# Second context's column sums from k-tiles added in 16 bits on GpSimd and VectorE, in place of 64 column-tiled matmuls

## The chip, the core and the metric

The kernel runs on one core of a Trainium2 chip. The metric is the device time of one execution in microseconds (us). Three runs of the kernel before gave 602.07, 602.37 and 602.42 us; the median is 602.37 us.

## The reference

Two residual blocks over x, of shape (2, 1024, 2048); each of the two batch entries has its own context of 2048 x 2048.

```python
def fake_quant(x, scale, zp):
    q = jnp.clip(jnp.round(x / s + z), 0.0, 255.0)
    return (q - z) * s
# first block: both operands quantised, then a matmul with the context
x = x + jnp.tanh(g_xattn[0]) * jnp.matmul(fake_quant(_layernorm(x)), fake_quant(ctx_4096))
# second block: a linear layer of rank 512
weight = U * S[None, :] @ V.T
x = x + jnp.tanh(g_ffn[0]) * jnp.einsum('bti,oi->bto', _layernorm(x), weight)
```

The zero points are not whole numbers that can be taken out beforehand, so the matmul runs on centred integers, which bf16 holds exactly, and the rest is repaired by a row correction and a column correction. The column correction needs, for each of the 2048 columns of a context, the sum over its 2048 rows (k) of the quantised context.

## The kernel before

**Tiling.** Rows of x go in 16 tiles (t or u, 0 to 15) of 128 rows; tiles 0 to 7 belong to the first context, 8 to 15 to the second. Columns go in four blocks n of 512. The contraction k has 16 tiles of 128. `q2` holds one quantised context in bf16, [128, 4, 16, 512]; the second overwrites the first. A context arrives in chunks of two k-tiles (128 x 1024): eight chunks to a column block, 32 to a context. Chunks are numbered 0 to 31 and 32 to 63. So the second context's blocks n = 0, 1, 2, 3 are chunks 32-39, 40-47, 48-55, 56-63.

**Stages of a tile.** `s1(t)` is the first matmul (four units of 16 matmuls, L556), `x1_unit` adds it to the rows in `ring`; `mm3(u)` (L587, L592) and `mm4(u)` (L653, L654, L658) are the two halves of the low-rank layer, with operands split in f16 high and low parts; `hid_hi`/`hid_lo` and `x_hi`/`x_lo` make those splits on ScalarE and VectorE; `y_unit` adds the result (L1207). Every engine's queue is written out by hand, in order; semaphores are the only ordering between engines.

**The second context.** ScalarE loads and rounds each chunk to uint8 into a ring `u8r` of eight places (`op1`, L757), and waits for the chunk eight earlier to have been converted. GpSimd converts each chunk to centred bf16 in `q2` (`op2`, L254); all 32 chunks of the second context are GpSimd's. ScalarE's last two roundings (chunks 62, 63) stand behind `hid_hi(7)`. After the 32 conversions GpSimd does `pre_row(8)` (L260) and `pre(8, n)` (L265).

**Its column sums.** On TensorE, between `mm4(6)` and `mm4(7)`, `colsum(1, n)` for n = 0, 1, 2 runs 48 matmuls in column-tiled form: ones of 128 x 32 against a k-tile, four k-tiles at a time into four groups of 32 partitions (L523). Block 3's 16 follow behind `mm4(7)`. Each bank then holds four partial sums. ScalarE and VectorE split them into f16 high and low parts (`column_parts` L840, `column_low` L1195) in `corr`, and `colsum_total` (L532, L533) adds the groups by two matmuls to a block: for blocks 0 to 2 inside `mm4(7)`, for block 3 behind the first unit of `s1(8)`. ScalarE writes the correction (`column_correction`, L851), which GpSimd adds to the rows of tiles 8 to 15.

**Order on VectorE around there:** `xT_copy(1)`, `quantise(8)` (L1107), `hid_lo(7)` (L1190), `row_correction(8)`, `y_unit(6, 0..3)` with `sums1(9)` and `variance1(9)` in between, `column_low(0..2)`, `quantise(9)`, `y_unit(7, 0..3)` and the rest of tiles 9 and 10.

Of the kernel before, what the change touches and what calls it, by code (L numbers as in the profile page):

```python
# [7 lines left out]
def gated_block_program(nc, x, ctx_in, params, U_t, S, V, out):  # L8
# [4 lines left out]
    P = 128  # L13
    NB, SEQ, D = x.shape
    RANK = V.shape[1]
    KT = D // P
    RT = RANK // P
    W = 512
# [5 lines left out]
    CQ = KT // CK  # L24
    CB = NQ * CQ
    R = 4
    G = 3
    NST = 10
    CG = 4
    GW = P // CG  # L30
    H_PE = (5,)
# [15 lines left out]
    with es:  # L47
# [98 lines left out]
        colsum_done = sem("colsum_done")  # L146
        parts_hi = sem("parts_hi")
        parts_lo = sem("parts_lo")
        colsum_summed = sem("colsum_summed")
        corr_ready = sem("corr_ready")  # L150
# [44 lines left out]
        unit_bank = lambda t, n: bank[4 * (n % 2) + t] if t < G else bank[(unit(t, n) - NQ * G) % 3]  # L195
        colsum_bank = lambda b, n: bank[4 * (n % 2) + 3] if b == 0 else bank[n]
        h_bank = lambda u: bank[3 + u % 2]
# [4 lines left out]
        y_bank = lambda i: bank[5 + i % 3]  # L202
        part_hi = lambda n: corr[:, n * W:n * W + W // 2].bitcast(f16)
        part_lo = lambda n: corr[:, n * W + W // 2:(n + 1) * W].bitcast(f16)
        chunk = lambda c: (c // CB, c % CB // CQ, c % CQ)
# [34 lines left out]
        def _(pool):  # L240
            def op2(c):
# [10 lines left out]
                if b > 0:  # L252
                    pool.wait_ge(s1_done, unit(TB * b - 1, n) + 1)
                nc.gpsimd.tensor_scalar(q2_chunk(c), u8r[:, c % NU8, :], C_NC2, 1.0, ALU.add, ALU.mult)\  # L254
                    .then_inc(q2_pool, 1)

            def pre_row(t):
                pool.wait_ge(q_u8, part_count(t))
                pool.wait_ge(row_ready, t + 1)
                nc.gpsimd.tensor_scalar(xt(t), xt(t), bvec[:, t % R, 1:2], 1.0, ALU.add, ALU.mult).then_inc(x1_row, 1)  # L260

            def pre(t, n):
# [10 lines left out]
                                    base=0, pattern=[[-1, P]], channel_multiplier=1).then_inc(ident_ready, 1)  # L273
            nc.gpsimd.memset(ones_h[:, :], 4.0 / GW).then_inc(setup_ready, 1)

# [12 lines left out]
            for t in range(G, NT):  # L288
                if t == TB:
                    for c in range(CB, 2 * CB):  # L290
                        op2(c)
                if t == G:
                    pool.wait_ge(t_written, 2 * G)
                    nc.gpsimd.memset(ident_h, 0.0).then_inc(ident_free, 1)
                    pool.wait_ge(ident_free, 1)
                    nc.gpsimd.affine_select(out=ident_h, in_=ident_h, compare_op=ALU.not_equal, fill=1.0, base=0,
                                            pattern=[[-1, P]], channel_multiplier=1).then_inc(ident_ready, 1)
                if t not in (6, 7):
                    pre_row(t)
                    for n in range(NQ):  # L300
                        pre(t, n)
                elif t == 6:
                    for v, n in MIXED:
                        if n == 0:
                            pre_row(v)
                        pre(v, n)
# [182 lines left out]
        def _(pe):  # L489
# [15 lines left out]

            def colsum(b, n, k0=0, k1=KT):
                if k0 == 0 and b == 0 and n >= 2:
                    pe.wait_ge(corr_ready, n - 1)
                if k0 == 0 and b > 0:
                    if n < NQ - 1:  # L510
                        pe.wait_ge(x1_ready, S1_END(TB - 1))
                    else:
                        pe.wait_ge(h_hi, TB - 1)
                        pe.wait_ge(h_lo, TB - 1)
                for k in range(k0, k1):
                    if k % CK == 0:
                        need_chunk(CB * b + CQ * n + k // CK)
                    if b == 0:
                        mm = nc.tensor.matmul(colsum_bank(b, n)[:, :], ones_b[:, :], q2[:, n, k, :],  # L519
                                              start=(k == 0), stop=(k == KT - 1))  # L520
                    else:
                        g = k % CG * GW
                        mm = nc.tensor.matmul(colsum_bank(b, n)[g:g + GW, :], ones_b[:, g:g + GW], q2[:, n, k, :],  # L523
                                              start=(k < CG), stop=(k >= KT - CG), tile_position=(0, g))
                if k1 == KT:
                    mm.then_inc(colsum_done, 1)

            def colsum_total(n):
                pe.wait_ge(setup_ready, 5)
                pe.wait_ge(parts_hi, n + 1)  # L530
                pe.wait_ge(parts_lo, n + 1)
                nc.tensor.matmul(colsum_bank(1, n)[:, :], ones_h[:, :], part_hi(n), start=True, stop=False)  # L532
                nc.tensor.matmul(colsum_bank(1, n)[:, :], ones_h[:, :], part_lo(n), start=False, stop=True)\  # L533
                    .then_inc(colsum_summed, 1)

# [83 lines left out]
            def mm4(u):  # L619
# [4 lines left out]
                for n in range(NQ):  # L624
# [8 lines left out]
                    if u == 0:  # L633
                        pe.wait_ge(split_hi, VP + RT * (n + 1))
                    if u == TB - 1 and n == 2:
                        for j in range(NQ - 1):
                            colsum_total(j)
                    t_hi, t_lo = hT_of(u)[:, 0:RT, :], hT_of(u)[:, RT:2 * RT, :]
# [35 lines left out]
            pe.wait_ge(ident_ready, 1)  # L674
            colsum(0, 0, 0, CK)
            q_pieces(0, 0)
            q_pieces(0, 1)
            colsum(0, 0, CK, 2 * CK)
            s1_part(0, 0, 0, 2 * CK)
            colsum(0, 0, 2 * CK, 3 * CK)  # L680
            s1_part(0, 0, 2 * CK, 3 * CK)
# [3 lines left out]
            for i in range(3, 7):  # L685
                if i == 6:
                    q_pieces(2, 0)
                colsum(0, 0, CK * i, CK * i + CK)
                for t in range(2):
                    s1_part(t, 0, CK * i, CK * i + CK)  # L690
            q_pieces(2, 1)
            s1_part(2, 0, 0, 7 * CK)
            colsum(0, 0, 7 * CK, KT)
            for t in range(G):
                s1_part(t, 0, 7 * CK, KT)
            for n in range(1, NQ):
                for i in range(CQ):
                    colsum(0, n, CK * i, CK * i + CK)
                    for t in range(G if n < NQ - 1 else 1):
# [29 lines left out]
            mm4(6)  # L729
            for n in range(NQ - 1):  # L730
                colsum(1, n)
            mm4(7)
            colsum(1, NQ - 1)
            s1_part(8, 0)
            colsum_total(NQ - 1)
            for n in range(1, NQ):
# [12 lines left out]
        def _(act):  # L749
# [84 lines left out]

            def column_parts(n):
                act.wait_ge(colsum_done, NQ + n + 1)
                act.wait_ge(x1_pre, unit(TB - 1, n) + 1)
                if n == 0:
                    act.wait_ge(ctx_u8, act_u8(CORR_CHUNK))
                nc.scalar.activation(part_hi(n), colsum_bank(1, n)[:, :], ACT.Copy, scale=0.25).then_inc(parts_hi, 1)  # L840

            def column_correction(b, n):
                if b > 0:
                    act.wait_ge(colsum_summed, n + 1)
                else:
                    act.wait_ge(colsum_done, n + 1)
                    if n == 0:
                        act.wait_ge(const_ready, 1)
                    elif n == NQ - 1:
                        act.wait_ge(smax_ready, 1)  # L850
                nc.scalar.activation(corr[:, n * W:(n + 1) * W], colsum_bank(b, n)[:, :], ACT.Identity,  # L851
# [158 lines left out]
            for n in range(NQ - 1):  # L1010
                column_parts(n)
            for n in range(NQ - 1):
                column_correction(1, n)
            op2(9)
            column_parts(3)
            column_correction(1, 3)
# [17 lines left out]
        def _(dve):  # L1034
# [130 lines left out]
            def x_lo_half(u, g):  # L1165
                mean, scale = ln2[:, u % 2, 0:1], ln2[:, u % 2, 8:9]
                if 2 * u + g > 0:
                    dve.wait_ge(xs_lo, 2 * u + g)
                if u == 6 and g == 0:
                    dve.wait_ge(ctx_u8, act_u8(XN_CHUNK))  # L1170
# [21 lines left out]

            def column_low(n):
                dve.wait_ge(parts_hi, n + 1)
                stt(part_lo(n), colsum_bank(1, n)[:, :], 0.25, part_hi(n), ALU.mult, ALU.subtract).then_inc(parts_lo, 1)  # L1195

# [186 lines left out]
            xT_copy(1)  # L1383
            quantise(8)
            hid_lo(7)
            row_correction(8)
            y_unit(6, 0)
            y_unit(6, 1)
            sums1(9)
            variance1(9)  # L1390
            y_unit(6, 2)
            y_unit(6, 3)
            column_low(0)
            column_low(1)
            column_low(2)
            quantise(9)
            y_unit(7, 0)
            y_unit(7, 1)
            row_correction(9)
            sums1(10)  # L1400
            y_unit(7, 2)
            y_unit(7, 3)
            column_low(3)
            variance1(10)
# [59 lines left out]
```

## Time and profile before

| | us |
|---|---|
| median of 3 runs (range) | 602.37 (602.07 to 602.42) |
| profiled execution: its span | 600.8 |
| TensorE matmuls busy | 583.0 (97%) |
| VectorE busy | 384.5 (64%) |
| ScalarE busy | 210.5 (35%) |
| GpSimd busy | 193.5 (32%) |

The profile gives the span of its execution, from the first instruction to the last. The time of the same execution is not listed apart; the median of the runs is 1.5 us above the span. Busy is the time in which an engine had an instruction under way. A matmul's record overlaps the next one's, so the distance between starts, not the record's length, is what one costs. "Idle before" a row is the gap ahead of it and the event that ended the gap.

### The profile page before, as it was taken

What the parts mean: (1) busy time and instruction counts of PE and PEld (TensorE: products, weight loads), DVE (VectorE), ACT (ScalarE), POOL (GpSimd) and SP (SyncE); (2) the same over time, 40 slices, a digit from 0 to 9 for tenths busy, and PEclk for the clock granted to TensorE, in tenths of its full rate; (3) what the DMA queues carried; (4) which work ended last, traced back from release to release, by engine and by line L of the source; (5) the groups of instructions that cost most, each with busy time, mean ns of one, the idle gap of its engine ahead of it and who ended that gap; (6) DMA issues with size and microseconds to landing.
All of it is one profiled execution on the core that took longest, in us unless ns stands there. A gap on an engine that the chain in (4) does not pass through costs nothing.

```text
span 600.8 us, 7536 instructions
## 1 busy us (share of the span) xinstructions
PE 583.0 (97%) x2800; PEld 266.3 (44%) x2800; DVE 384.5 (64%) x703; ACT 210.5 (35%) x256; POOL 193.5 (32%) x149
## 2 busy tenths in 40 slices
PE   1999999999999999999999999999999999999998
PEld 0444444444444444445444444444444444444444
DVE  6968999995288962855266975647375665735212
ACT  4799877822041432476422220303011030301000
POOL 2998850002223419735505800210404030030000
PEclk9999999999999999999999999999999999999999
DMA  8999995539828896979934432360917355171512
GB/s 275 387 387 386 308 262 127 109 122 196 242 54 230 192 217 189 274 264 327 235 123 140 102 73 54 75 189 12 211 42 157 106 97 166 32 161 35 123 53 105
DMA packets 145940, 102.74 MB, mean 171 GB/s; under 512 B 108784, under 2 KB 109040, under 8 KB 145904
## 3 DMA queue, kind: packets, MB, share of 16 engines
q1 hardware_dynamic: 136912, 84.96, 53.6%
q10 hardware_dynamic: 8992, 17.30, 8.8%
q8 instruction: 22, 0.36, 0.2%
q14 instruction: 14, 0.11, 0.1%
HBM read 58.99 MB, written 16.78 MB: 126 GB/s over the span
## 4 chain that ended last, share of the span: by engine, by line
PE 74%; DVE 12%; DMA 7%; issue 3%; ACT 1%; SPq 1%; POOL 1%; ACTq 0%; DVEq 0%
PE bank L556 27%; PE bank L587 14%; PE bank L654 8%; PE bank L653 8%; PE bank L658 8%; PE bank L592 7%; DMA v_hl<-in_ctx_dram 4%; DVE u_hl L1249 2%; DVE ring L1134 2%; DVE xn L1171 1%; DVE xs L1174 1%; DVE v_hl L1243 1%; DMA qT<-qn 1%; PE bank L519 1%; DMA ring<-in_x_dram 1%
## 5 line engine op out<-in xcount | busy, mean ns | idle before, releaser
L556 PE MATMUL bank<-q,qT 128*128 128x512 bf16 x896 | 202.1, 381 | 0.6 <-DVE ring L1134 0.3
L556 PEld LDWEIGHTS bank<-q,qT 128*128 128x128 bf16 x896 | 87.7, 98 | 107.9 <-issue 1.8
L260 POOL TENSOR_SCALAR ring<-ring,bvec 128x2048 f32<-128x2048 f32 x16 | 33.3, 2084 | 270.2 <-DVE bvec L1116 270.2
L587 PE MATMUL bank<-v_hl,xT 128*128 128x512 f16 x512 | 115.8, 379 | 0.0
L265 POOL TENSOR_TENSOR ring<-ring,corr 128x512 f32<-128x512 f32 x64 | 88.7, 1417 | 24.6 <-ACT corr L851 23.6
L1134 DVE SCALAR_TENSOR_TENSOR ring<-bank,const,ring 128x512 f32<-128x512 f32 x64 | 47.6, 743 | 57.9 <-PE bank L556 57.8
L1207 DVE SCALAR_TENSOR_TENSOR ring<-bank,cy,ring 128x512 f32<-128x512 f32 x63 | 46.6, 747 | 56.7 <-PE bank L658 56.6
L654 PE MATMUL bank<-u_hl,hbuf 128*128 128x512 f16 x208 | 78.9, 380 | 0.0
L653 PE MATMUL bank<-u_hl,hbuf 128*128 128x512 f16 x208 | 78.9, 379 | 0.0
L254 POOL TENSOR_SCALAR q<-u8r,const 128x1024 bf16<-128x1024 uint8 x52 | 64.2, 1243 | 39.2 <-ACT u8r L757 35.6
L587 PEld LDWEIGHTS bank<-v_hl,xT 128*128 128x128 f16 x512 | 49.9, 98 | 59.9 <-DMA xT<-xs 0.5
L798 ACT ACTIVATE ln<-ln,const 128x1 f32<-128x1 f32 x16 | 4.7, 294 | 189.8 <-DVE ln L1147 189.8
L592 PE MATMUL bank<-v_hl,xT 128*128 128x512 f16 x256 | 60.5, 379 | 0.0
L658 PE MATMUL bank<-u_hl,hbuf 128*128 128x512 f16 x208 | 53.4, 379 | 0.0
L1174 DVE TENSOR_TENSOR xs<-xn,xs 128x1024 f16<-128x1024 f32 x32 | 46.8, 1461 | 5.3 <-ACT xs L812 4.3
L1136 DVE BATCH_NORM_STATS2 st<-ring 128x6 f32<-128x512 f32 x64 | 44.5, 695 | 2.2
L1075 DVE BATCH_NORM_STATS2 st<-ring 128x6 f32<-128x512 f32 x64 | 40.4, 680 | 8.2 <-DMA ring<-in_x_dram 8.1
L812 ACT ACTIVATE xs<-ring,ln 128x1024 f16<-128x1024 f32 x32 | 38.2, 1232 | 14.8 <-DVE ln L1159 14.8
L592 PEld LDWEIGHTS bank<-v_hl,xT 128*128 128x128 f16 x256 | 25.1, 98 | 30.2
L784 ACT ACTIVATE qn<-qn,const 128x2048 bf16<-128x2048 uint8 x13 | 26.0, 2002 | 29.3 <-DVE qn L1107 29.3
L1190 DVE SCALAR_TENSOR_TENSOR hbuf<-bank,hbuf 128x512 f16<-128x512 f32 x16 | 11.0, 686 | 34.3 <-ACT hbuf L826 34.3
L519 PE MATMUL bank<-q,ones_b 128*128 128x512 bf16 x64 | 20.4, 402 | 12.7 <-POOL q L254 12.1
(136 smaller groups left out, 524.9 us busy)
## 6 DMA issues: line engine op xcount, KB each, us to landing
out_dram<-ring SPq DMA_DIRECT2D x63, 256.0 KB, 3.6
ring<-in_x_dram SPq DMA_DIRECT2D x62, 256.0 KB, 4.1
v_hl<-in_ctx_dram SPq DMA_DIRECT2D x26, 512.0 KB, 11.5
stage<-in_ctx_dram ACTq DMA_DIRECT2D x17, 512.0 KB, 5.5
u_hl<-in_L_ffn_V_dram SPq DMA_DIRECT2D x8, 512.0 KB, 11.4
corr<-in_ctx_dram ACTq DMA_DIRECT2D x8, 512.0 KB, 6.1
stage<-in_ctx_dram SPq DMA_DIRECT2D x6, 512.0 KB, 11.4
q<-in_ctx_dram ACTq DMA_DIRECT2D x4, 512.0 KB, 10.1
```

Of the source, the lines that this page charges most:

```text
L254: nc.gpsimd.tensor_scalar(q2_chunk(c), u8r[:, c % NU8, :], C_NC2, 1.0, ALU.add, ALU.mult)\
L265: nc.gpsimd.tensor_tensor(xq(t, n), xq(t, n), corr[:, n * W:(n + 1) * W], ALU.add).then_inc(x1_pre, 1)
L556: mm = nc.tensor.matmul(unit_bank(t, n)[:, :], qT_of(t)[:, k, :], q2[:, n, k, :], start=(k == 0), stop=(k == KT - 1))
L587: nc.tensor.matmul(h_bank(u)[:, :], xT[:, g, half, k % 8, :], v_hl[:, k, 0, :], start=(g == 0 and a == 0 and half == 0), stop=False)
L592: mm = nc.tensor.matmul(h_bank(u)[:, :], xT[:, g, 0, k % 8, :], v_hl[:, k, 1, :], start=False, stop=(g == 1 and a == 7))
L653: nc.tensor.matmul(y_bank(i)[:, :], t_hi[:, r, :], u_hl[:, n, r, 0, :], start=(r == 0), stop=False)
L654: nc.tensor.matmul(y_bank(i)[:, :], t_lo[:, r, :], u_hl[:, n, r, 0, :], start=False, stop=False)
L658: mm = nc.tensor.matmul(y_bank(i)[:, :], t_hi[:, r, :], u_hl[:, n, r, 1, :], start=False, stop=(r == RT - 1))
L1134: stt(xq(t, n), unit_bank(t, n)[:, :], C_A, xq(t, n), ALU.mult, ALU.add).then_inc(x1_ready, 1)
L1136: nc.vector.bn_stats(st2[:, t % R, n, :], xq(t, n)).then_inc(st2_ready, 1)
L1174: tt(xs[:, g, 1, :], xn[:, :], xs[:, g, 0, :], ALU.subtract).then_inc(xs_lo, 1)
L1207: stt(xq(u, n), y_bank(i)[:, :], cy[:, n:n + 1], xq(u, n), ALU.mult, ALU.add).then_inc(y_ready, 1)
```

## The change

The 64 column-tiled matmuls and the split in parts go. Instead the eight chunks of a column block are added element by element into one 128 x 1024 sum in f16 (seven additions to a block; a chunk's two k-tiles stay side by side), and two full-width matmuls with ones add the two halves and the 128 partitions. GpSimd makes the sums of blocks 0 and 1: after each conversion of a chunk of blocks 2 and 3 except the first of each, it adds a chunk of block 0 or 1. VectorE makes those of blocks 2 and 3. The sums lie in `xn` (blocks 0, 1) and in the low halves of `xs` (blocks 2, 3). On TensorE the sums of blocks 0, 1, 2 stand between `mm4(6)` and `mm4(7)`, that of block 3 behind the first unit of `s1(8)`. VectorE's `sums1(9)`, `variance1(9)`, `quantise(9)`, `row_correction(9)` and `sums1(10)` move by a place or two.

The index in `k_sum` reads c = CB + CQ * n + i, the chunk i of block n. In GpSimd's loop the call has n = 0 while chunks 48 to 55 are converted and n = 1 while chunks 56 to 63 are.

```diff
+    KS = CQ - 1
+        k_sums = lambda n: xn[:, n * W:n * W + W].bitcast(f16) if n < 2 else xs[:, n // 3, 0, :]
...
+            def k_sum(n, i):                                   # GpSimd
+                c = CB + CQ * n + i
+                if i == 1:
+                    pool.wait_ge(q2_pool, pool_count(c))
+                    pool.wait_ge(xs_lo, 2 * TB)
+                else:
+                    pool.wait_ge(k_summed_pool, KS * n + i - 1)
+                nc.gpsimd.tensor_tensor(k_sums(n), q2_chunk(c - 1) if i == 1 else k_sums(n), q2_chunk(c), ALU.add)\
+                    .then_inc(k_summed_pool, 1)
...
-            nc.gpsimd.memset(ones_h[:, :], 4.0 / GW).then_inc(setup_ready, 1)
+            nc.gpsimd.memset(ones_h[:, :], 1.0).then_inc(setup_ready, 1)
...
                     for c in range(CB, 2 * CB):
                         op2(c)
+                        if c >= CB + 2 * CQ and c % CQ > 0:
+                            k_sum((c - CB) // CQ - 2, c % CQ)
...
-            def colsum_total(n):
+            def colsum_of_sums(n):                             # TensorE
                 pe.wait_ge(setup_ready, 5)
+                if n < 2:
+                    pe.wait_ge(k_summed_pool, KS * (n + 1))
+                else:
+                    pe.wait_ge(k_summed, KS * (n - 1))
+                if n < 2:
+                    pe.wait_ge(xT_copied, 4)
+                else:
+                    pe.wait_ge(h_hi, TB - 1 + n - 2)
+                    pe.wait_ge(h_lo, TB - 1 + n - 2)
+                for a in range(CK):
+                    mm = nc.tensor.matmul(colsum_bank(1, n)[:, :], ones_h[:, :], k_sums(n)[:, a * W:(a + 1) * W],
+                                          start=(a == 0), stop=(a == CK - 1))
+                mm.then_inc(colsum_done, 1)
...
-                    if u == TB - 1 and n == 2:
-                        for j in range(NQ - 1):
-                            colsum_total(j)
...
             mm3(7)
             mm4(6)
-            for n in range(NQ - 1):
-                colsum(1, n)
+            colsum_of_sums(0)
+            colsum_of_sums(1)
+            colsum_of_sums(2)
             mm4(7)
-            colsum(1, NQ - 1)
             s1_part(8, 0)
-            colsum_total(NQ - 1)
+            colsum_of_sums(3)
...
-            def column_parts(n):                               # ScalarE
             def column_correction(b, n):
+                act.wait_ge(colsum_done, NQ * b + n + 1)
+                if b > 0:
+                    act.wait_ge(x1_pre, unit(TB - 1, n) + 1)
+                    if n == 0:
+                        act.wait_ge(ctx_u8, act_u8(CORR_CHUNK))
...
-            def column_low(n):                                 # VectorE
+            def k_sum(n, i):
+                c = CB + CQ * n + i
+                dve.wait_ge(q2_pool, pool_count(c))
+                if i == 1:
+                    dve.wait_ge(xT_written, 2 + 2 * (n // 3))
+                else:
+                    dve.wait_ge(k_summed, KS * (n - 2) + i - 1)
+                tt(k_sums(n), q2_chunk(c - 1) if i == 1 else k_sums(n), q2_chunk(c), ALU.add).then_inc(k_summed, 1)
...
             xT_copy(1)
             quantise(8)
+            k_sum_part(2, 1, 4)
             hid_lo(7)
             row_correction(8)
             y_unit(6, 0)
+            k_sum_part(2, 4, 6)
             y_unit(6, 1)
+            k_sum_part(2, 6)
+            y_unit(6, 2)
             sums1(9)
             variance1(9)
-            y_unit(6, 2)
             y_unit(6, 3)
-            column_low(0)
-            column_low(1)
-            column_low(2)
+            k_sum_part(3, 1, 4)
+            y_unit(7, 0)
+            k_sum_part(3, 4, 6)
             quantise(9)
-            y_unit(7, 0)
             y_unit(7, 1)
+            k_sum_part(3, 6)
+            y_unit(7, 2)
             row_correction(9)
+            y_unit(7, 3)
             sums1(10)
-            y_unit(7, 2)
-            y_unit(7, 3)
-            column_low(3)
```

`k_sum_part(n, a, b)` calls `k_sum(n, i)` for i from a to b - 1 (to 7 where b is left out). `x_lo_half(8, 0)` gets a wait for all eight column sums, since `xn` is its room.

## Rows read from the trace of the kernel before

**Rows 1.** The page, parts 1 and 2: engine totals, and TensorE's granted clock by slice.

```profile
PE 583.0 (97%) x2800; PEld 266.3 (44%) x2800; DVE 384.5 (64%) x703; ACT 210.5 (35%) x256; POOL 193.5 (32%) x149
...
PEclk9999999999999999999999999999999999999999
```

**Rows 2.** Waits of TensorE over the span: total us, times, longest us.

```profile
PE bank L519 <- POOL q L254: 12.1, 2, 11.3
...
PE bank L556 <- DVE ring L1134: 0.3, 1, 0.3
```

**Rows 3.** Timeline of TensorE: start us, us, instruction, [idle before].

```profile
304.16 1.03 PE L658 MATMUL bank<-u_hl,hbuf 128*128 128x512 f16 x4
305.12 2.77 PE L523 MATMUL bank<-q,ones_b 128*32 128x512 bf16 x48
307.82 0.39 PE L653 MATMUL bank<-u_hl,qT 128*128 128x512 f16 x1
...
318.62 1.03 PE L658 MATMUL bank<-u_hl,qT 128*128 128x512 f16 x4
319.58 1.05 PE L523 MATMUL bank<-q,ones_b 128*32 128x512 bf16 x16
320.56 3.63 PE L556 MATMUL bank<-q,qT 128*128 128x512 bf16 x16
```

**Rows 4.** Timeline of GpSimd through the last conversions of the second context.

```profile
266.57 1.12 POOL L254 TENSOR_SCALAR q<-u8r,const 128x1024 bf16<-128x1024 uint8 x1 [3.48 <-ACT u8r L757]
268.32 1.12 POOL L254 TENSOR_SCALAR q<-u8r,const 128x1024 bf16<-128x1024 uint8 x1 [0.63 <-ACT u8r L757]
...
286.91 3.17 POOL L254 TENSOR_SCALAR q<-u8r,const 128x1024 bf16<-128x1024 uint8 x2 [0.63 <-ACT u8r L757]
296.68 2.25 POOL L254 TENSOR_SCALAR q<-u8r,const 128x1024 bf16<-128x1024 uint8 x2 [6.60 <-ACT u8r L757]
```

**Rows 5.** Timeline of ScalarE: the rounding of chunk 49.

```profile
265.25 1.23 ACT L757 ACTIVATE u8r<-corr,par,const 128x1024 uint8<-128x1024 f32 x1
```

**Rows 6.** Single lines on GpSimd: duration ns min/median/max, first and last start, form.

```profile
L265 POOL TENSOR_TENSOR ring<-ring,corr x64: 1260/1271/2255, 42.7 to 530.1; 128x512 f32<-128x512 f32 x64
...
L254 POOL TENSOR_SCALAR q<-u8r,const x52: 1111/1118/2077, 10.1 to 297.8; 128x1024 bf16<-128x1024 uint8 x52
...
L260 POOL TENSOR_SCALAR ring<-ring,bvec x16: 1971/1972/2515, 32.2 to 524.4; 128x2048 f32<-128x2048 f32 x16
```

**Rows 7.** Timeline of GpSimd at the start: a conversion that waits for its predecessor.

```profile
13.81 1.19 POOL L245 TENSOR_SCALAR u8r<-v_hl,const,par 128x1024 uint8<-128x1024 f32 x1 [2.62 <-DMA v_hl<-in_ctx_dram]
15.09 1.12 POOL L254 TENSOR_SCALAR q<-u8r,const 128x1024 bf16<-128x1024 uint8 x1
```

**Rows 8.** Single lines on VectorE, columns as in rows 6.

```profile
L1174 DVE TENSOR_TENSOR xs<-xn,xs x32: 1224/1226/2872, 82.3 to 552.9; 128x1024 f16<-128x1024 f32 x32
...
L1184 DVE COPY xT<-bank x4: 681/682/692, 272.8 to 284.9; 128x1024 f16<-128x1024 f16 x4
```

**Rows 9.** Timelines of GpSimd and VectorE where both are at work.

```profile
336.72 6.38 POOL L265 TENSOR_TENSOR ring<-ring,corr 128x512 f32<-128x512 f32 x4
...
339.79 2.18 DVE L1174 TENSOR_TENSOR xs<-xn,xs 128x1024 f16<-128x1024 f32 x1
```

**Rows 10.** Timeline of VectorE in the stretch of the new additions.

```profile
265.45 1.22 DVE L1174 TENSOR_TENSOR xs<-xn,xs 128x1024 f16<-128x1024 f32 x1 [1.81 <-ACT xs L812]
...
286.65 1.34 DVE L1107 TENSOR_SCALAR qn<-ring,ln 128x2048 uint8<-128x2048 f32 x1
295.49 0.69 DVE L1190 SCALAR_TENSOR_TENSOR hbuf<-bank,hbuf 128x512 f16<-128x512 f32 x1 [7.49 <-ACT hbuf L826]
```

**Rows 11.** Timeline of TensorE at its start.

```profile
17.10 1.91 PE L556 MATMUL bank<-q,qT 128*128 128x512 bf16 x4
...
20.65 1.63 PE L496 MATMUL bank<-ident_b,qn 128*128 128x128 bf16 x16
22.82 1.47 PE L556 MATMUL bank<-q,xT 128*128 128x512 bf16 x6 [0.54 <-ACT xT L789]
```

More of the change, by code:

```diff
@@ L28, in gated_block_program @@
     NST = 10
-    CG = 4
-    GW = P // CG
     H_PE = (5,)
@@ L146, in gated_block_program @@
         colsum_done = sem("colsum_done")
-        parts_hi = sem("parts_hi")
-        parts_lo = sem("parts_lo")
-        colsum_summed = sem("colsum_summed")
+        k_summed = sem("k_summed")
+        k_summed_pool = sem("k_summed_pool")
         corr_ready = sem("corr_ready")
@@ L195, in gated_block_program @@
         unit_bank = lambda t, n: bank[4 * (n % 2) + t] if t < G else bank[(unit(t, n) - NQ * G) % 3]
-        colsum_bank = lambda b, n: bank[4 * (n % 2) + 3] if b == 0 else bank[n]
+        colsum_bank = lambda b, n: bank[4 * (n % 2) + 3] if b == 0 else bank[(0, 1, 3, 4)[n]]
         h_bank = lambda u: bank[3 + u % 2]
@@ L202, in gated_block_program @@
         y_bank = lambda i: bank[5 + i % 3]
-        part_hi = lambda n: corr[:, n * W:n * W + W // 2].bitcast(f16)
-        part_lo = lambda n: corr[:, n * W + W // 2:(n + 1) * W].bitcast(f16)
+        k_sums = lambda n: xn[:, n * W:n * W + W].bitcast(f16) if n < 2 else xs[:, n // 3, 0, :]
         chunk = lambda c: (c // CB, c % CB // CQ, c % CQ)
@@ L504, in need_chunk, with colsum @@
                     pe.wait_ge(q2_pool, pool_count(c))
-            def colsum(b, n, k0=0, k1=KT):
-                if k0 == 0 and b == 0 and n >= 2:
+            def colsum(n, k0=0, k1=KT):
+                if k0 == 0 and n >= 2:
                     pe.wait_ge(corr_ready, n - 1)
[L509 to L514, printed above, removed]
@@ L515, in colsum @@
                 for k in range(k0, k1):
                     if k % CK == 0:
[L517 to L524, printed above, removed]
+                        need_chunk(CQ * n + k // CK)
@@ L525, in colsum @@
+                    mm = nc.tensor.matmul(colsum_bank(0, n)[:, :], ones_b[:, :], q2[:, n, k, :],
+                                          start=(k == 0), stop=(k == KT - 1))
                 if k1 == KT:
                     mm.then_inc(colsum_done, 1)
-            def colsum_total(n):
+            def colsum_of_sums(n):
                 pe.wait_ge(setup_ready, 5)
[L530 to L534, printed above, removed]
+                if n < 2:
[11 more added lines that the diff above has]
+                mm.then_inc(colsum_done, 1)
@@ L674, in _ @@
             pe.wait_ge(ident_ready, 1)
-            colsum(0, 0, 0, CK)
+            colsum(0, 0, CK)
             q_pieces(0, 0)
             q_pieces(0, 1)
-            colsum(0, 0, CK, 2 * CK)
+            colsum(0, CK, 2 * CK)
             s1_part(0, 0, 0, 2 * CK)
-            colsum(0, 0, 2 * CK, 3 * CK)
+            colsum(0, 2 * CK, 3 * CK)
             s1_part(0, 0, 2 * CK, 3 * CK)
@@ L687, in _ @@
                     q_pieces(2, 0)
-                colsum(0, 0, CK * i, CK * i + CK)
+                colsum(0, CK * i, CK * i + CK)
                 for t in range(2):
@@ L692, in _ @@
             s1_part(2, 0, 0, 7 * CK)
-            colsum(0, 0, 7 * CK, KT)
+            colsum(0, 7 * CK, KT)
             for t in range(G):
@@ L697, in _ @@
                 for i in range(CQ):
-                    colsum(0, n, CK * i, CK * i + CK)
+                    colsum(n, CK * i, CK * i + CK)
                     for t in range(G if n < NQ - 1 else 1):
@@ L833, in hT_copy @@
                     .then_inc(hT_copied, 1)
-            def column_parts(n):
[L836 to L840, printed above, removed]
             def column_correction(b, n):
+                act.wait_ge(colsum_done, NQ * b + n + 1)
                 if b > 0:
-                    act.wait_ge(colsum_summed, n + 1)
-                else:
-                    act.wait_ge(colsum_done, n + 1)
+                    act.wait_ge(x1_pre, unit(TB - 1, n) + 1)
                     if n == 0:
-                        act.wait_ge(const_ready, 1)
-                    elif n == NQ - 1:
-                        act.wait_ge(smax_ready, 1)
+                        act.wait_ge(ctx_u8, act_u8(CORR_CHUNK))
+                elif n == 0:
+                    act.wait_ge(const_ready, 1)
+                elif n == NQ - 1:
+                    act.wait_ge(smax_ready, 1)
                 nc.scalar.activation(corr[:, n * W:(n + 1) * W], colsum_bank(b, n)[:, :], ACT.Identity,
@@ L1010, in _ @@
             for n in range(NQ - 1):
-                column_parts(n)
-            for n in range(NQ - 1):
                 column_correction(1, n)
             op2(9)
-            column_parts(3)
             column_correction(1, 3)
@@ L1168, in x_lo_half @@
                     dve.wait_ge(xs_lo, 2 * u + g)
+                if u == TB and g == 0:
+                    dve.wait_ge(colsum_done, 2 * NQ)
                 if u == 6 and g == 0:
@@ L1191, in hid_lo, with k_sum_part @@
                     .then_inc(h_lo, 1)
-            def column_low(n):
-                dve.wait_ge(parts_hi, n + 1)
-                stt(part_lo(n), colsum_bank(1, n)[:, :], 0.25, part_hi(n), ALU.mult, ALU.subtract).then_inc(parts_lo, 1)
+            def k_sum(n, i):
[6 more added lines that the diff above has]
+                tt(k_sums(n), q2_chunk(c - 1) if i == 1 else k_sums(n), q2_chunk(c), ALU.add).then_inc(k_summed, 1)
+            def k_sum_part(n, a=1, b=CQ):
+                for i in range(a, b):
+                    k_sum(n, i)
             def y_unit(u, n):
```

## The prediction

> **What bounds the kernel now.** I read the page's totals first, then TensorE's waits, then the timelines of the four engines between 255 and 345 us. TensorE is busy 97% of the span at a full granted clock [rows 1]. Its waits say more: nearly all of its waiting is 12.1 us for the first conversion at the very start, and behind 300 us the only wait is 0.3 us for VectorE's L1134 [rows 2]. So in the stretch of the change, and from there to the end, matmuls stand back to back. What is taken off TensorE there comes off the time, and what makes it wait is added; nothing later has slack in which a delay could vanish, except that 0.3 us. GpSimd is busy 32% over the span, but that is an average, and its own stretch must be read.
>
> **What TensorE saves.** The last matmul ahead of the 48 column-tiled ones starts its group of four at 304.16; a pitch of 0.216 us (16 matmuls take 3.63 us with a last record of 0.38) puts the next start at 305.02. `mm4(7)` starts at 307.82, so the 48 cost 2.80 us, or 0.058 us each, gap included. The other 16 lie between 318.62 + 0.86 = 319.48 and 320.56: 1.08 us [rows 3]. Sum removed: 3.88 us. The matmuls that finish the sums were two to a block, eight in all, and are eight again: 8 x 0.216 = 1.73 us before and after. If nothing waits, the gain is 3.9 us. The four ScalarE and four VectorE instructions that split the parts ran beside TensorE; taking them away is worth nothing.
>
> **What GpSimd gets.** Fourteen additions of 128 x 1024, and TensorE waits for the fourteenth right behind `mm4(6)`, at 305.02 + 0.43. This is the step that decides. It takes two quantities, the start and the pace.
>
> Start: the first addition follows the conversion of chunk 49, which is the one at 266.57, when its uint8 chunk is there [rows 4, 5]. It ends at 267.69. The other wait of that addition, for `x_lo(7)`, is met at 265.45 + 1.22 = 266.67 [rows 10], so it costs nothing. Two of the fourteen additions wait for the instruction just ahead of them; such a wait left 0.09 us between an end and the next start [rows 7]. The other twelve wait for an addition that is one conversion older. Waits: 0.2 us.
>
> Pace of an addition: the trace has no 16-bit two-input instruction on GpSimd. The nearest is L265, also a tensor by tensor addition, 1.26 to 1.27 us for 512 columns of f32. Two one-input forms give the fixed part: 1.118 us at 1024 columns and 1.971 at 2048, so 0.833 us per 1024 columns and 0.27 us fixed [rows 6]. The two forms have different types (uint8 to bf16, f32 to f32) and lie on one plausible line, so width in bytes seems not to count. Taking the fixed part off L265 leaves 1.00 us for 512 columns, and 1024 take 2.00 + 0.27 = 2.27; with no fixed part at all it would be 2 x 1.26 = 2.52. I take 2.30. The lower bound is the case that two 16-bit elements pass at a time: 1.00 + 0.27 = 1.27 us.
>
> The Trainium skill ("GPSIMD Engine Reference", section 3.1) speaks of about 2.6 cycles per element for a two-input addition, because both inputs share one read port; its 4.50 us for 2048 columns of f32 and the 1.26 us here would make an estimate of 2.34 us for 1024. It states no 16-bit figure, so it speaks for the case that I take without excluding the other.
>
> Conversions: chunks 50 to 63 are fourteen, at a pitch of 1.10 us (the last two in 2.25 less nothing between them, [rows 4]): 15.4 us. Today GpSimd waits between them for ScalarE; with an addition behind each, 3.4 us to a pair against ScalarE's 1.75 us (the distance of the conversions at 266.57 and 268.32), GpSimd no longer waits. The last two chunks can't be converted before 296.68, since ScalarE rounds them behind `hid_hi(7)`; GpSimd reaches them later than that. ScalarE's roundings wait for the chunk eight earlier: chunk 63 would wait for chunk 55, converted near 290 with the delays below, ahead of its 296. So loads and `hid_hi(7)` are not held up.
>
> Without disturbance GpSimd ends at 267.7 + 0.2 + 14 x 2.30 + 15.4 = 315.5.
>
> Disturbance by VectorE: at 336.72 four L265 take 6.38 us where four of 1.26 are 5.04, and VectorE's L1174 beside them takes 2.18 instead of 1.22 [rows 8, 9]. The 1.3 us lost on GpSimd is about one L1174: they take turns. So each of VectorE's new additions costs GpSimd its own length. The trace has none in 16 bits. An f32 one of 1024 columns takes 1.224 us, a 16-bit copy of 1024 columns 0.682 [rows 8]; I take 0.69 by type and keep 1.22 as the upper end. Ten of the fourteen fall beside GpSimd's run: the seven of block 2 (behind `quantise(8)`, from 288 on) and the first three of block 3; the last four stand behind `y_unit(7, 0)`, which waits for TensorE. `quantise(8)` costs about 0.9: at 286.91 two conversions took 3.17 us instead of 2.24, just beside its 1.34 us [rows 4, 10]. Sum 10 x 0.69 + 0.9 = 7.8; I take 7.2, since a turn can fall into a gap that is there anyway. The bounds are 0 and 10 x 1.22 + 1.3 = 13.5. End of GpSimd: 322.7.
>
> On turn-taking the Trainium skill ("SBUF — State Buffer", "Who interferes with whom") says that a VectorE instruction with two SBUF inputs contends with a GpSimd one that reads SBUF, as an exclusive lock; the 2.18 against 1.22 us agrees. It is a rule against this change, because the two engines now do such additions in the same stretch.
>
> **What TensorE does then.** Sums of block 0 run at 305.0; block 1's wait until 322.8, blocks 1 and 2 take four matmuls, 0.86 us, and `mm4(7)` starts at 323.7 instead of 307.82: 15.8 us later. From there 6 x 0.216 = 1.30 us of totals inside `mm4(7)` and 1.08 us of column-tiled matmuls are gone, so `s1(8)` starts 13.5 us later, at 334.0. Queued behind the waiting matmul is all of TensorE's work, `mm4(7)`, `s1(8)` and so on; there is nothing that it could do meanwhile.
>
> Clock: at the start of the span, after 11 us without work, matmuls of 512 columns come 0.425 us apart ((1.91 - 0.635) / 3, the slow record being 0.635), which is the level of 1.2 GHz, and from 22.82 on 0.218 apart, the level of 2.4 GHz, though the page's throttle row shows full clock throughout [rows 1, 11]. From 17.10 to 22.28 TensorE worked almost without a break at the lower level; half of 5.2 us is 2.6 us lost. The trace has no long idle stretch in the middle of the span, so whether 17 us of idling cools it is open: between 0 and 2.6, I take 2.0.
>
> **VectorE and ScalarE.** VectorE's additions wait for turns on GpSimd, perhaps 2 us each. `hid_lo(7)` stands behind three of them, from 288 to near 295.5, where it is due [rows 10]; `y_unit(6, 1)` and its followers slip by a few us, and TensorE needs their banks two units later. While TensorE waits for GpSimd to 322.8, all of this is covered; if GpSimd were fast, the additions would also take turns of half the length. Block 3's last additions end near 334, its matmuls stand at 337.5. The conversions are never held up by VectorE's additions except through the turns counted above. Behind `s1(8)` the order is the old one, shifted. ScalarE loses four instructions of 0.6 us and gains none. No DMA is added. SP's transpose of tile 9 and loads behind it wait for `y_done` of `mm4(7)` as before, and shift with it. All of this: 0.
>
> **The sum.** 15.8 - 1.30 - 1.08 + 2.0 = +15.4. On the profiled execution's span of 600.8 that is 616.2; the median of the runs is 1.5 us above that span, so 617.8 us.
>
> **Rivals.**
> A. *Two 16-bit elements at a time on GpSimd.* Additions of 1.27 us: GpSimd ends at 267.9 + 14 x 1.27 + 15.4 = 301.1 without turns, and the whole 3.9 us come: 598.5. With 7 us of turns it ends at 308.1; `mm4(7)` starts at 309.1, 1.2 later, less 2.38: -1.1, 601.2. The turning point is an end at 309.2 (309.2 + 0.96 - 307.82 = 2.38): 1.35 us per addition with all turns, or 1.85 without. For it: 16-bit data is half the bytes. Against: in rows 6 bytes make no difference. This is the case on the other side: 598.5 to 601.3. Chance 0.14.
> B. *No turns lost.* VectorE's 16-bit additions slip in at no price for GpSimd: end at 315.5, TensorE +6.3, with the clock +8.3: 610.7. For it: the ten additions are short. Against: rows 9. Chance 0.15.
> C. *Slow turns.* Additions of 2.52 us and VectorE's in 1.22 us: end at 267.9 + 35.3 + 15.4 + 13.5 = 332.1, +22.9, with 2.6 for the clock +25.5: 627.9. Chance 0.11.
> D. *The clock does not fall* while TensorE waits: the forecast less 2.0, 615.8. This lies inside the forecast's own case, which has 0.60 (613.5 to 622.5).
>
> **How the numbers follow.** The likeliest is 617.8. The range 604.0 to 626.0 holds the forecast's case, B and part of C, and leaves out A and the far end of C, about 0.2. A measurement of this kernel tells about 0.2% (1.2 us) from no change. Faster by more than that is the better part of A, 0.10; within 0.2% is its rest, 0.05, with a little for additions between 1.3 and 1.6 us; slower is all else, 0.85.
>
> **What would show it.** In the changed profile: L265-like additions on GpSimd of bf16 at 2.3 us (forecast), 1.3 (A); their chain from 267.7 to 322.7; one wait of TensorE of some 17 us for GpSimd between `mm4(6)` and `mm4(7)`, the largest of the list after the start; VectorE's additions of 0.69 us alone and 2 to 3 us in turn; matmuls 0.43 us apart for some us behind the wait; and `s1(8)` at about 336. I am wrong if that wait is missing, if additions run under 1.8 us, or if later idle time of TensorE (SP's loads, VectorE) appears that is not in this sum.

## The result, and the profile after

| | before | after |
|---|---|---|
| median, us (range, runs) | 602.39 (602.07 to 602.75, 4) | 612.99 (612.61 to 613.62, 4) |
| ratio, 95% interval | | 1.0179 (1.0166 to 1.0192) |
| span of the profiled execution | 600.8 | 611.0 |
| TensorE busy / GpSimd busy | 583.0 / 193.5 | 578.9 / 227.4 |

The change makes the kernel 10.6 us slower, by the median; the spans differ by 10.2 us. The forecast was 617.8 us, range 604.0 to 626.0.

The page after, part 1, and from part 2 TensorE, GpSimd and the granted clock by slice (against [rows 1]):

```profile
PE 578.9 (95%) x2707; PEld 265.1 (43%) x2736; DVE 403.5 (66%) x713; ACT 207.9 (34%) x252; POOL 227.4 (37%) x163
...
PE   1899999999999999999919999999999999999998
...
POOL 2899840003032448669991910040404021040000
PEclk9999999999999999999959999999999999999999
```

One slice of TensorE is nearly empty (305.5 to 320.8 us), and the granted clock dips in it. GpSimd is full in that slice and in the two ahead of it. TensorE's waits after (against [rows 2]):

```profile
PE bank L521 <- POOL q L251: 12.9, 3, 11.2
PE bank L538 <- issue: 12.4, 1, 12.4
```

L538 is the matmul of `colsum_of_sums`. The profile calls what ended the wait "issue", since it found no releaser; the timelines supply it. TensorE after (against [rows 3]):

```profile
303.95 1.03 PE L661 MATMUL bank<-u_hl,hbuf 128*128 128x512 f16 x4
304.81 0.59 PE L538 MATMUL bank<-xn,ones_h 128*128 128x512 f16 x2
317.83 1.01 PE L538 MATMUL bank<-xn,ones_h 128*128 128x512 f16 x2 [12.43 <-issue]
318.64 1.06 PE L538 MATMUL bank<-xs,ones_h 128*128 128x512 f16 x2
319.49 0.63 PE L656 MATMUL bank<-u_hl,qT 128*128 128x512 f16 x1
319.92 0.63 PE L657 MATMUL bank<-u_hl,qT 128*128 128x512 f16 x1
...
321.50 0.38 PE L657 MATMUL bank<-u_hl,qT 128*128 128x512 f16 x1
...
329.91 1.03 PE L661 MATMUL bank<-u_hl,qT 128*128 128x512 f16 x4
330.99 3.40 PE L562 MATMUL bank<-q,qT 128*128 128x512 bf16 x15
```

Block 0's sum runs at 304.81, block 1's only at 317.83. (Of the 16 matmuls that begin `s1(8)` one record is missing; the unit starts at 329.91 + 0.86 = 330.77.) GpSimd after, the start, a stretch with VectorE's additions, and the end (against [rows 4]):

```profile
266.73 1.12 POOL L251 TENSOR_SCALAR q<-u8r,const 128x1024 bf16<-128x1024 uint8 x1 [3.84 <-ACT u8r L760]
267.81 2.12 POOL L261 TENSOR_TENSOR xn<-q 128x1024 f16<-128x1024 bf16 x1
269.91 1.12 POOL L251 TENSOR_SCALAR q<-u8r,const 128x1024 bf16<-128x1024 uint8 x1
270.99 2.12 POOL L261 TENSOR_TENSOR xn<-xn,q 128x1024 f16<-128x1024 f16 x1
...
289.02 3.63 POOL L251 TENSOR_SCALAR q<-u8r,const 128x1024 bf16<-128x1024 uint8 x2
292.62 2.55 POOL L261 TENSOR_TENSOR xn<-q 128x1024 f16<-128x1024 bf16 x1
295.15 1.55 POOL L251 TENSOR_SCALAR q<-u8r,const 128x1024 bf16<-128x1024 uint8 x1
...
315.62 2.11 POOL L261 TENSOR_TENSOR xn<-xn,q 128x1024 f16<-128x1024 f16 x1
```

No row in the chain has idle time in front: GpSimd never waits between 267.81 and 317.73, and 0.10 us after its last addition TensorE goes on. Undisturbed, an addition costs 2.10 us (distance of starts) and a conversion 1.08. From 289 on the same two forms also take 2.55 and 1.55 us, 0.43 more: four additions and five conversions. VectorE there:

```profile
286.44 3.70 DVE L1101 TENSOR_SCALAR qn<-ring,ln 128x2048 uint8<-128x2048 f32 x1
290.06 1.60 DVE L1196 TENSOR_TENSOR xs<-q 128x1024 f16<-128x1024 bf16 x1
291.77 3.95 DVE L1196 TENSOR_TENSOR xs<-xs,q 128x1024 f16<-128x1024 f16 x2
...
323.88 1.48 DVE L1196 TENSOR_TENSOR xs<-xs,q 128x1024 f16<-128x1024 f16 x2
```

Two of its additions take 1.48 us when GpSimd is free and 3.95 beside it; `quantise(8)` (L1101) goes from 1.34 to 3.70.

### The profile page after: what moved, and what is told of

Its sections match the earlier page's. It is cut to its first block, busy times and chain, and to the rows that moved or that the text cites. A ratio compares the mean times of both kernels' runs of the same rounds, so it can differ in the third digit from the quotient of the medians.

```text
span 611.0 us, 7413 instructions
## 1 busy us (share of the span) xinstructions
PE 578.9 (95%) x2707; PEld 265.1 (43%) x2736; DVE 403.5 (66%) x713; ACT 207.9 (34%) x252; POOL 227.4 (37%) x163
## 4 chain that ended last, share of the span: by engine, by line
PE 84%; DVE 6%; issue 4%; DMA 2%; POOL 1%; SPq 1%; ACT 0%; DVEq 0%
PE bank L562 29%; PE bank L593 16%; PE bank L656 9%; PE bank L657 9%; PE bank L661 9%; PE bank L598 8%; PE bank L521 2%; DMA v_hl<-in_ctx_dram 2%; DVE v_hl L1248 1%; DVE xs L1170 1%; DVE xn L1167 1%; SPq L322 1%; DVE ring L1128 1%; POOL u8r L242 1%; DMA xT<-xs 1%
## 5 line engine op out<-in xcount | busy, mean ns | idle before, releaser
L562 PE MATMUL bank<-q,qT 128*128 128x512 bf16 x873 | 199.1, 381 | 1.6 <-DVE ring L1128 0.3
L1212 DVE SCALAR_TENSOR_TENSOR ring<-bank,cy,ring 128x512 f32<-128x512 f32 x63 | 46.7, 746 | 61.6 <-PE bank L661 61.6
L251 POOL TENSOR_SCALAR q<-u8r,const 128x1024 bf16<-128x1024 uint8 x52 | 66.7, 1292 | 24.3 <-ACT u8r L760 20.7
L760 ACT ACTIVATE u8r<-stage,par,const 128x1024 uint8<-128x1024 f32 x23 | 28.3, 1235 | 11.0 <-ACT u8r L760 4.5
```

What stands on the lines that cost most here:

```text
L562: mm = nc.tensor.matmul(unit_bank(t, n)[:, :], qT_of(t)[:, k, :], q2[:, n, k, :], start=(k == 0), stop=(k == KT - 1))
L1212: stt(xq(u, n), y_bank(i)[:, :], cy[:, n:n + 1], xq(u, n), ALU.mult, ALU.add).then_inc(y_ready, 1)
```

## The experiments

Each ratio is against the kernel before on the same chip (medians there 601.97 us for the first four, 601.91 for the last three).

| run | us, median (range) | ratio, 95% interval |
|---|---|---|
| e1_late_sums | 603.62 (603.26 to 605.26) | 1.0033 (1.0020 to 1.0047) |
| e2_dve_tiny | 609.89 (609.70 to 610.49) | 1.0131 (1.0114 to 1.0148) |
| e3_pool_tiny | 598.71 (598.15 to 599.60) | 0.9947 (0.9933 to 0.9962) |
| e4_pool_half | 598.12 (597.79 to 598.48) | 0.9936 (0.9922 to 0.9951) |
| e5_dummies | 610.62 (610.47 to 611.00) | 1.0145 (1.0132 to 1.0159) |
| e6_late_y_first | 605.07 (604.34 to 605.14) | 1.0049 (1.0033 to 1.0064) |
| e7_shared_out | 598.61 (597.98 to 598.81) | 0.9943 (0.9931 to 0.9956) |

**GpSimd's additions shortened to 16 columns, and to 512.**

```diff
+                a, b, d = q2_chunk(c - 1) if i == 1 else k_sums(n), q2_chunk(c), k_sums(n)
+                w = CK * W if i == 1 else 16      # e4: else W
-                nc.gpsimd.tensor_tensor(k_sums(n), ..., q2_chunk(c), ALU.add)
+                nc.gpsimd.tensor_tensor(d[:, 0:w], a[:, 0:w], b[:, 0:w], ALU.add)
```

> GpSimd's additions but the first of each block are cut to 16 of 1024 columns (its sums are left out). Theory: TensorE's wait vanishes and with it the slow clock; what is left is the saving of 3.9 us: 598.5 us. Rival (VectorE's additions are late for mm4(7) or for the sum of block 2): 600 to 603 us, with a wait of TensorE for VectorE in place of that for GpSimd.

> GpSimd's additions but the first of each block are cut to 512 of 1024 columns (half of its sums is left out). Theory (GpSimd's time goes by elements and not by bytes): a 16-bit addition of 512 columns takes about 1.2 us, near the 1.26 us of the f32 one of 512 columns; twelve are 0.92 us shorter each, GpSimd ends near 306.5, TensorE waits some 1 us, 600 us. Rival (bytes count: f32 at 512 columns is 2 KB a partition, 16 bits half of that): 0.75 us each, no wait, 598.5 us.

With 16 columns the kernel is 3.3 us faster than before: take GpSimd's length away and the loss is gone and most of the 3.9 us is there, with VectorE's additions in place. The rival (VectorE late) did not happen: TensorE has no wait between `mm4(6)` and `s1(8)`. With 512 columns TensorE's wait is 0.3 us and the kernel 3.9 us faster, 1.9 better than the 600 expected. GpSimd reached its end at 305.1 and not 306.5, so the wait is 0.7 us shorter than expected and matmuls stay 0.216 us apart behind it; what makes up the rest of the 1.9 was not separated. One addition of this run, and the wait:

```profile
271.28 1.15 POOL L263 TENSOR_TENSOR xn<-xn,q 128x512 f16<-128x512 f16 x1
```

```profile
PE bank L539 <- issue: 0.3, 1, 0.3
```

1.15 us for 512 columns and 2.12 for 1024 are 1.9 ns a column and 0.18 us fixed. The f32 addition of 512 columns takes 1.26 [rows 6]. So with half the bytes 9% less time: apart from that 9%, time goes by elements; the rival's 0.75 us is out.

**VectorE's additions shortened to 16 columns.**

```diff
-                tt(k_sums(n), ..., q2_chunk(c), ALU.add).then_inc(k_summed, 1)
+                a, b, d = q2_chunk(c - 1) if i == 1 else k_sums(n), q2_chunk(c), k_sums(n)
+                if i == 1:
+                    tt(d, a, b, ALU.add).then_inc(k_summed, 1)
+                else:
+                    tt(d[:, 0:16], a[:, 0:16], b[:, 0:16], ALU.add).then_inc(k_summed, 1)
```

> VectorE's additions but the first of each block are cut to 16 of 1024 columns (its sums are left out). Theory (VectorE's additions take turns with GpSimd and delay it by 0.43 us each): GpSimd's chain ends near 313 instead of 317.7, the kernel is 4 to 5 us faster than the changed one, 608.5 us. Rival (the conversions of 1.55 and additions of 2.55 us come from GpSimd itself, or from DMA): GpSimd's durations stay, 613 us.

GpSimd in this run; the first row is beside `quantise(8)` and VectorE's first full addition, the fourth beside its other full one:

```profile
289.33 3.63 POOL L251 TENSOR_SCALAR q<-u8r,const 128x1024 bf16<-128x1024 uint8 x2
292.92 2.12 POOL L261 TENSOR_TENSOR xn<-q 128x1024 f16<-128x1024 bf16 x1
295.02 1.12 POOL L251 TENSOR_SCALAR q<-u8r,const 128x1024 bf16<-128x1024 uint8 x1
...
307.77 1.55 POOL L251 TENSOR_SCALAR q<-u8r,const 128x1024 bf16<-128x1024 uint8 x1
...
312.47 2.11 POOL L261 TENSOR_TENSOR xn<-xn,q 128x1024 f16<-128x1024 f16 x1
```

Where VectorE's additions were cut, GpSimd's rows are back at 2.12 and 1.12; where a full one is left, 0.43 us is left. So the 0.43 us is VectorE's turn. Eight cut turns are 3.4 us; GpSimd ends 3.15 us earlier, having begun 0.3 later. In time it is +7.9 us against before, where the change has +10.6: 2.7 us gained, less than the 4 to 5 expected. Two turns of full additions and that of `quantise(8)` stay, so the chain ends 3.15 us earlier and not 4.7. And the clock takes more: TensorE waits 9.4 us here instead of 12.4, and behind the wait the matmuls are slow for longer.

```profile
314.68 1.01 PE L538 MATMUL bank<-xn,ones_h 128*128 128x512 f16 x2 [9.44 <-issue]
...
319.33 0.61 PE L657 MATMUL bank<-u_hl,qT 128*128 128x512 f16 x1
319.75 1.05 PE L661 MATMUL bank<-u_hl,qT 128*128 128x512 f16 x4
```

Twelve matmuls take 5.07 us (314.68 to 319.75) where 0.216 us apart they would take 2.6: 2.5 us lost, against 1.7 in the changed kernel. So the clock's price is no fixed number for a wait.

**TensorE kept at work during its wait.**

```diff
             colsum_of_sums(0)
+            pe.wait_ge(q2_pool, pool_count(CB))
+            for _ in range(52):
+                nc.tensor.matmul(bank[2][:, :], ones_b[:, :], q2[:, 0, 0, :], start=True, stop=True)
             colsum_of_sums(1)
```

> The changed kernel with 52 matmuls more, whose result nobody reads, between TensorE's sums of blocks 0 and 1, that is inside its wait for GpSimd (11.2 us of work in a wait of 12.4). Theory (part of the loss is that TensorE's clock falls during the wait and stays low for 3.4 us behind it, which costs half of that): the wait shrinks to about 1 us at the same end, matmuls stand 0.216 us apart behind it, the kernel is 1.7 us faster than the changed one, 611.3 us. Rival (the wide distances behind the wait are a drain of the queue or the weights): 613 us.

```profile
304.83 11.39 PE L736 MATMUL bank<-q,ones_b 128*128 128x512 bf16 x52
317.72 0.59 PE L538 MATMUL bank<-xn,ones_h 128*128 128x512 f16 x2 [1.51 <-issue]
```

The pair behind the wait takes 0.59 us instead of 1.01, and the kernel is 1.9 us faster than the changed one (+8.7 against +10.6 over before). More matmuls, less time: the clock had been part of the loss. The rival is out.

**TensorE's sums moved behind `s1(8, 0)`.** The same kernel, another order; blocks 1 and 2 aren't needed before `s1(8, 1)`.

```diff
             colsum_of_sums(0)
-            colsum_of_sums(1)
-            colsum_of_sums(2)
             mm4(7)
             s1_part(8, 0)
+            colsum_of_sums(1)
+            colsum_of_sums(2)
             colsum_of_sums(3)
...
-                        if t == TB and n == 0:
-                            pe.wait_ge(corr_ready, 2 * NQ - 1)
+                        if t == TB and n in (1, 2):
+                            pe.wait_ge(corr_ready, NQ + n)
...
-            for n in range(NQ - 1):
-                column_correction(1, n)
+            column_correction(1, 0)
             op2(9)
-            column_correction(1, 3)
+            for n in range(1, NQ):
+                column_correction(1, n)
```

> TensorE's sums of blocks 1 and 2 move from ahead of mm4(7) to behind the first unit of s1(8); ScalarE's corrections follow suit. Theory (the loss is TensorE's wait for GpSimd's fourteenth addition at 317.7, and only that): by 317.7 TensorE is in s1(8, 0), so the wait of 12.4 us and the slow stretch behind it vanish and the 3.9 us of column-tiled matmuls come through. VectorE becomes late: y_unit(7, 0) stands behind three additions that end at 314.7, and the fourth unit of mm4(7) wants it at 313.0, some 2.4 us. So 602.4 - 3.9 + 2.4 = 600.9 us. Rival (the additions slow the kernel elsewhere too, by port turns or held-up conversions): 604 us or more.

TensorE's waits here:

```profile
PE bank L656 <- DVE ring L1212: 3.6, 1, 3.6
PE bank L562 <- DVE ring L1128: 1.5, 2, 1.1
```

The wait of 12.4 us is gone and so are 9 of the 10.6 us, but the kernel doesn't gain; 603.62 us lies between my 600.9 and the rival's 604, and each has a part. In the profiled execution (605.26 us, 1.6 above the median) TensorE waits 3.6 us for `y_unit(7, 0)` (L1212), behind three additions of VectorE that take 2.65 and 3.94 us beside GpSimd, and 1.5 us for `x1_unit` behind `s1(8)`. The place was right, the size 1.2 us too small, and I had no term for `x1_unit` and for a second dip of the clock. Next, with `y_unit(7, 0)` first:

```diff
             y_unit(6, 3)
-            k_sum_part(3, 1, 4)
             y_unit(7, 0)
-            k_sum_part(3, 4, 6)
-            quantise(9)
+            k_sum_part(3, 1, 6)
             y_unit(7, 1)
+            quantise(9)
             k_sum_part(3, 6)
```

> As the first experiment (sums of blocks 1 and 2 behind the first unit of s1(8)), and y_unit(7, 0) ahead of VectorE's additions of block 3. Theory (what the first experiment lost was TensorE's 3.6 us for y_unit(7, 0), some 1 us of low clock behind it, and 1.5 us for VectorE behind s1(8)): the first two go, VectorE stays late behind s1(8), since its work is the same: 599.5 us. Rival (the waits behind s1(8) grow by what is won ahead of it, since VectorE is the bound there): 602 to 604 us.

My expectation of 599.5 failed; 605.07 is even above the rival's 604. TensorE, and VectorE ahead of it:

```profile
319.84 0.59 PE L538 MATMUL bank<-xs,ones_h 128*128 128x512 f16 x2
325.17 1.01 PE L538 MATMUL bank<-xs,ones_h 128*128 128x512 f16 x2 [4.74 <-issue]
```

```profile
311.50 8.00 DVE L1196 TENSOR_TENSOR xs<-xs,q 128x1024 f16<-128x1024 f16 x4
...
322.52 2.55 DVE L1196 TENSOR_TENSOR xs<-xs,q 128x1024 f16<-128x1024 f16 x2
```

The wait moved on to block 3's sum: four additions cost VectorE 2.0 us each beside GpSimd, where two alone take 1.48, and the last one ends at 325.07. While GpSimd adds until 318.9, VectorE is the bound of this stretch, and neither of the two orders tried helps. A part of the 4.7 us is my order, though: between the four additions and the last two stand `y_unit(7, 1)` and `quantise(9)`, from 319.42 to 322.60. An order with the last two additions ahead of them was not run.

**GpSimd with seven additions instead of fourteen.** VectorE makes block 0's sum as well: five of its additions in mostly idle time from 267 us on, the last two behind `quantise(8)`.

```diff
-                        if c >= CB + 2 * CQ and c % CQ > 0:
-                            k_sum((c - CB) // CQ - 2, c % CQ)
+                        if CB + 2 * CQ < c < CB + 3 * CQ:
+                            k_sum(1, c % CQ)
...
             x_lo_half(7, 1)
+            k_sum_part(0, 1, 5)
             xT_copy(0)
             hid_lo(6)
             y_unit(5, 0)
+            k_sum_part(0, 5, 6)
             y_unit(5, 1)
...
             quantise(8)
+            k_sum_part(0, 6)
             k_sum_part(2, 1, 4)
```

> GpSimd makes the sum of block 1 alone (seven additions, behind the conversions of chunks 49 to 55), VectorE makes that of block 0 too, in its idle stretches from 267 to 290 us; TensorE's order is that of the changed kernel. Theory (the change fails on GpSimd's length alone): GpSimd reaches its last conversion at the time of the kernel before, near 299, TensorE waits for neither, and the 3.9 us come: 598.5 us, faster than before by 0.6%. Rival (VectorE's 21 additions push hid_lo(7) or y_unit past what TensorE needs): 600 to 604 us.

598.61 us, as expected: 3.3 us faster than before and 14 us faster than the changed kernel. GpSimd's last seven additions are gone, and the six matmuls of blocks 0 to 2 stand without a gap:

```profile
267.90 2.56 POOL L261 TENSOR_TENSOR xn<-q 128x1024 f16<-128x1024 bf16 x1
...
293.25 11.80 POOL L251 TENSOR_SCALAR q<-u8r,const 128x1024 bf16<-128x1024 uint8 x8
305.03 1.97 POOL L267 TENSOR_SCALAR ring<-ring,bvec 128x2048 f32<-128x2048 f32 x1
```

```profile
304.57 1.03 PE L538 MATMUL bank<-xn,ones_h 128*128 128x512 f16 x4
305.43 0.59 PE L538 MATMUL bank<-xs,ones_h 128*128 128x512 f16 x2
```

The sum comes out so: 3.9 us of column-tiled matmuls less, and 0.4 us more of waiting for `x1_unit` (0.7 in two waits, where before had 0.3 in one), which makes 3.5; 3.3 were measured. GpSimd ends its conversions only at 305.0, not near 299 as I wrote: it took turns with the fourteen additions of blocks 0 and 2 and with `quantise(8)`, in the early stretch too (the first row above). TensorE doesn't ask for that end, so it cost nothing.

## Why the prediction was right, point by point

**The step that decides** held: GpSimd's chain starts at 267.8 (267.7 forecast), has no gap, and TensorE waits for its fourteenth addition. Shown by the timelines and by the run that shortens those additions.

**Pace of an addition:** 2.30 us forecast, 2.10 measured from start to start. The nearest value by the f32 form was 2.27, and 2.10 is 7% below it; at 512 columns, e4_pool_half has 16 bits 9% below f32. This is 14 x 0.20 = 2.8 us of the miss. The estimate of 2.34 us, from the f32 figure of the Trainium skill ("GPSIMD Engine Reference", section 3.1), is a tenth above the 2.12 us that a 16-bit addition takes here. The statement there that the two inputs of an addition share one read port, and that this sets its pace, agrees with 2.12 us for 1024 columns against 1.12 for a conversion of the same size, which has one input; that the port is the reason isn't shown, since the two differ in operation and types as well. Rival A (1.27 us) is out, and so is the 2.52 us of rival C.

**Turns:** 7.2 forecast. Measured are nine of 0.43 us and 1.4 us around `quantise(8)` and the first addition: 5.3. The step was right and its size was off: I had charged GpSimd the whole length of VectorE's addition, 0.69 us, and it loses 0.43. That they meet ten times was right. Of the miss this is 1.9 us. Rival B (no turns) is out by e2_dve_tiny, and the turns of 1.22 us of rival C with it.

**TensorE:** `mm4(7)` starts at 319.49 instead of 307.82, 11.7 us later (15.8 forecast). The 1.30 and 1.08 us come off as forecast.

**Clock:** 2.0 forecast. Behind the wait 512 columns stand 0.42 to 0.43 us apart, the level of 1.2 GHz, from 317.83 to 321.20, and 0.216 apart, 2.4 GHz, from 321.50; half of 3.4 us is 1.7. Rival D (no fall) is out. That a value taken between 0 and 2.6 came within 0.3 us is partly luck: e2_dve_tiny lost 2.5 us behind a shorter wait.

**Sum:** 11.7 + 0.9 (the part of the clock's loss behind 319.49) - 1.30 - 1.08 = 10.2, the difference of the spans. Against the forecast's 15.4 the 5 us missing are 2.8 of pace, 1.9 of turns, 0.3 of clock; about 0.2 remains. All of the miss is size, and all on one side: 612.99 lies in the range, and 0.5 us below the bounds (613.5 to 622.5) that I gave to the likeliest case.

**VectorE and ScalarE at 0:** right in this kernel, where TensorE's wait covers them. The clause that VectorE would take shorter turns if GpSimd were fast is borne out by e4_pool_half, where two take 2.98 us instead of 3.95. But e1 and e6 show what that cover was worth: without the wait, and with GpSimd's fourteen additions in place, the kernel stays 5.6 and 7.1 us above what before less 3.9 us would be, and TensorE's waits for VectorE (5.1 us in the profile of e1, 4.7 in that of e6) are the largest part of it.

## What to carry to other kernels

Work moved off a bounding engine is paid at the place where that engine next asks for its result: add up the helper's whole chain from its first possible start, not its idle share over the span. Two helpers that added at the same time slowed each other here, the one that the bounding engine waits for by 0.43 us a meeting; price the meetings, and first of all keep that helper's chain short. e7_shared_out won by halving the chain, and its meetings in the earlier stretch cost as much each. And when a wait is moved rather than its cause shortened, look for the next engine in line first: here VectorE's `y_unit(7, 0)` ended at 316.4, nearly as late as GpSimd's 317.7 in the changed kernel.

## What was not expected of the hardware

- GpSimd takes nearly as long for a 16-bit addition as for an f32 one of the same number of elements: 1.15 against 1.26 us at 512 columns; 0.22 us at 16 columns.
- In a turn, GpSimd loses 0.43 us to a VectorE 16-bit addition that takes 0.68 to 0.75 us alone, while VectorE loses more: its additions take 1.5 to 2.0 us each instead of 0.74.
- A wait of 12.4 us in the middle of the span cost TensorE another 1.7 us at the lower clock; e5_dummies got 1.9 us back with matmuls whose result nobody reads. A wait of 9.4 us (e2_dve_tiny) cost 2.5 us.
